# Splitting the values matmuls of an attention quad into two pieces, in a two-layer transformer kernel on one Trainium2 core

## The reference

```python
dots = jnp.einsum('bhid,bhjd->bhij', q, k) * scale
attn = jax.nn.softmax(jnp.where(mask, -jnp.inf, dots), axis=-1)
out = jnp.einsum('bhij,bhjd->bhid', attn, v)
x = _layernorm(x + out @ w_out + b_out)
x = _layernorm(x + ffn(x))
```

## Time and profile before

| what | us |
|---|---|
| runs of the kernel before | 1175.50, 1175.59, 1180.28 (median 1175.59) |
| the profiled execution | 1173.83 |
| its span, first to last instruction | 1172.1 |
| TensorE matmuls busy | 1027.9 |
| VectorE busy | 723.9 |
| ScalarE busy | 594.7 |
| GpSimd busy | 323.8 |

### The profile page before, as it was taken

One profiled execution on the slowest core, in us unless ns is written; L12 is line 12 of the kernel. 1 busy time (PEld: TensorE's weight loads), 2 busy tenths in 40 slices (PEclk: granted clock), 3 DMA queues, 4 the chain that ended last, 5 costly groups with the idle time before them and its releaser, 6 DMA issues. The chain is left out here.

```text
span 1172.1 us, 17910 instructions
## 1 busy us (share of the span) xinstructions
PE 1027.9 (88%) x6546; PEld 516.7 (44%) x6546; DVE 723.9 (62%) x1563; ACT 594.7 (51%) x1169; POOL 323.8 (28%) x391
## 2 busy tenths in 40 slices
PE   7947999999988899765779899999999988899996
PEld 4511233333324788742022333334333334488885
DVE  3767877777734655464878677777777724134322
ACT  3412667666665433234026576767777765523220
POOL 1041111111111343302135613315133150334331
PEclk9966999999999999878569999999999999999998
DMA  7585044444000000008922505235051000000001
GB/s 272 130 155 63 6 51 55 55 55 56 2 1 1 2 1 1 1 19 172 220 102 72 116 2 116 75 42 114 4 117 34 1 2 1 1 1 18 18 1 37
DMA packets 32980, 64.20 MB, mean 55 GB/s; under 512 B 6079, under 2 KB 22351, under 8 KB 30516
## 3 DMA queue, kind: packets, MB, share of 16 engines
q1 hardware_dynamic: 31004, 58.07, 24.9%
q0 software_dynamic: 1072, 3.80, 0.9%
q10 hardware_dynamic: 816, 1.18, 0.3%
HBM read 50.45 MB, written 12.32 MB: 54 GB/s over the span
## 5 line engine op out<-in xcount | busy, mean ns | idle before, releaser
L802 ACT ACTIVATE prob<-ps 128x512 f32<-128x512 f32 (+6 forms) x896 | 445.9, 535 | 306.1 <-PE ps L838 297.9
L838 PE MATMUL ps<-qop,kop 98*128 98x512 bf16 (+15 forms) x1376 | 311.8, 291 | 38.1 <-ACT prob L802 23.0
L824 PE MATMUL ps<-kop,qop 96*128 96x512 bf16 (+3 forms) x896 | 272.6, 380 | 53.1 <-DVE maxes L743 24.7
L838 PEld LDWEIGHTS ps<-qop,kop 107*128 107x128 bf16 (+2 forms) x1376 | 114.0, 98 | 311.7 <-ACT prob L802 236.7
L865 PE MATMUL ps<-prob,vst 128*32 128x512 f32 (+4 forms) x1792 | 212.1, 545 | 3.3 <-POOL prob L692 2.6
L743 DVE CUSTOM_DVE_ANT_0 attn<-ps,alibi_table 128x960 bf16<-128x960 f32 x128 | 148.0, 1156 | 86.6 <-PE ps L824 57.9
L692 POOL TENSOR_TENSOR prob<-prob,keep 128x384 int32<-128x384 int32 (+2 forms) x144 | 122.0, 849 | 276.1 <-ACT prob L802 273.5
L1207 PE MATMUL ps<-xs,ffn_parts 128*128 128x512 f32 x640 | 150.4, 392 | 4.5 <-DVE hf L1181 2.3
L743 DVE CUSTOM_DVE_ANT_0 tri<-ps,alibi_table 128x960 bf16<-128x960 f32 x128 | 147.6, 1153 | 3.0 <-PE ps L824 3.0
L824 PEld LDWEIGHTS ps<-kop,qop 96*128 96x128 bf16 x896 | 77.5, 100 | 143.4 <-DVE maxes L743 84.3
L1207 PEld LDWEIGHTS ps<-xs,ffn_parts 128*128 128x128 f32 x640 | 119.0, 188 | 29.7 <-DVE hf L1181 3.1
(11 more groups left out here) (97 smaller groups left out, 706.5 us busy)
## 6 DMA issues: line engine op xcount, KB each, us to landing
alibi_table<-in_table SPq DMA_DIRECT2D x32, 464.0 KB, 5.6
qop<-q_parts SPq DMA_DIRECT2D x96, 128.0 KB, 7.1
kop<-k_parts SPq DMA_DIRECT2D x48, 128.0 KB, 7.8
kop<-k_parts SPq DMA_DIRECT2D x48, 96.0 KB
q_parts<-qop SPq DMA_DIRECT2D x8, 384.0 KB, 3.0
q_parts<-kop SPq DMA_DIRECT2D x8, 384.0 KB, 6.5
x<-in_x SPq DMA_DIRECT2D x4, 512.0 KB, 7.2
out<-x SPq DMA_DIRECT2D x4, 512.0 KB, 2.9
```

The costliest lines, as they stand in the source:

```text
L802: nc.scalar.activation(prob[0:rows, q % 2, k % HG, lo % CH:lo % CH + hi - lo], ps[0:rows, T_BANK + k % 2, lo % CH:lo % CH + hi - lo], ACT. ...
L824: last = nc.tensor.matmul(ps[:, S_BANK + 2 * (k % S_SLOTS) + a // CH, a % CH:a % CH + b - a], qop[0:RD, par, h, i0:i0 + P], kop[0:RD, par, ...
L838: return nc.tensor.matmul(ps[0:rows, T_BANK + k % 2, a % CH:a % CH + b - a], lhs, rhs, start=start, stop=True, skip_group_check=True)
```

## The change

The values step of a quad is cut in two by query columns. `values0` does the first half of the columns, behind the third exponent step of the next quad and the score tiles due there, ahead of the fourth. It has the waits that the values step had: for the exponents, the masks and, where a sum is opened, the eviction. `values` does the second half where the values step stood, without a wait of its own, and raises `values_done`. The matmul that opens a sum, and the 64 small ones of the second layer, belong to the first piece. At the very end of a layer both pieces follow each other.

```diff
@@ -143,6 +143,10 @@
             upto = given_next + -(-(due_next - given_next) // (HG - h))
             steps += [("max", u, later) for u, later in stream_next[given_next:upto]]
             given_next = upto
+            if h == HG - 2 and n >= 1:
+                steps.append(("values0", n - 1, 0))
+            elif h == HG - 2 and late:
+                steps.append(("values0", nq - 1, -1))
         if n == 0 and late:
             steps += [(what, k, -1) for what, k in tail[:2]]
         if n == 1 and late:
@@ -161,7 +165,7 @@
         if n == rows_at and stream:
             steps.append(("rows", 0, 1))
     if last:
-        steps += [(what, k, 0) for what, k in tail]
+        steps += [("values0", nq - 1, 0)] + [(what, k, 0) for what, k in tail]
         steps = with_preparation(steps, nq)
     return steps
 
@@ -848,12 +852,14 @@
                         start = False
                 return last
 
-            def values(qd, par):
+            def values(qd, par, part):
 
                 half, kt = quads[qd]
                 lo, hi = columns_of(L, half, kt)
+                middle = (lo + hi) // 2
+                lo, hi = (lo, middle) if part == 0 else (middle, hi)
                 vt_ = kt if key_tile(L, kt)[1] == P else TB
-                opening = qd == 0 or quads[qd - 1][0] != half
+                opening = part == 0 and (qd == 0 or quads[qd - 1][0] != half)
                 uniform = opening and i == 1 and half == 0
                 if uniform:
 
@@ -901,6 +907,8 @@
                             pe.wait_ge(exp_done, n * NX + (k - 1))
                         shifted(k, b).then_inc(t_full, 1)
                     elif what == "values":
+                        values(k, b, 1).then_inc(values_done, 1)
+                    elif what == "values0":
                         half = quads[k][0]
                         if k > 0 and half != quads[k - 1][0]:
 
@@ -912,7 +920,7 @@
                         pe.wait_ge(exp_done, n * NX + HG * (k + 1))
                         if diagonal[k] is not None:
                             pe.wait_ge(masked, HG // MH * (n * upto[-1] + upto[k]))
-                        values(k, b).then_inc(values_done, 1)
+                        values(k, b, 0)
                     elif what == "norm":
                         pe.wait_ge(evicted, n * 2 + (k + 1))
```

## The result

The changed kernel took 1196.95, 1198.73 and 1210.12 us, against a median of 1175.76 us before: slower, ratio 1.0213 with a 95% interval of 1.0132 to 1.0295, which lies above 1 but does not settle whether it is 2% or more. A fourth run of 1263.25 us, at a mean granted clock of 0.813 where the others have 0.93 to 0.94, is left out of the ratio; with it the median of the runs is 1204.42 us. The profiled execution took 1196.95 us, 23.1 more than the 1173.83 of the one before, at the same granted clock (0.942 in both).

A forecast was written before the change was run, and what follows sets the result against it. TensorE was taken to bound both attention stages. Second layer +7.1 and first layer +14.3 made 21.4 us on the profiled 1173.83 us; with the runs' median 1.76 us higher, 1195.2 to 1197.0, stated as 1195, range 1181 to 1206.

The forecast's parts named there:

- The second edge: Extra entry to and exit from the values matmuls on TensorE: plus 0.10 and 0.14, about 0.24 us in every quad.
- What the piece fills: TensorE's wait for ScalarE between shifted 2 and shifted 3: minus 0.21 us, leaving +0.03 in an ordinary second-layer quad.
- The first layer, behind the third tile: Piece fills nothing behind the third score tile: nine quads (narrow last included) at 0.24, three at 0.03; 2.25 us a group.
- Group 6 of the first layer: First-layer group whose last four quads have no score tiles: allowed 6 x 0.24 and a little, 1.5 us.
- its last group: First layer's last group: about zero, with 0.5 us allowed for its 128-column quads.
- group 0 of the second layer: 32 score tiles over 13 quads, five quads with a values piece getting a third tile: plus 1.9 us.
- groups 1 to 6 of the second layer: Fourteen quads at 0.03 and two at 0.22 make 0.86 us a group: plus 5.2 us together.
- VectorE absorbs it: Rival, 0.13: VectorE limits first-layer quads with a third tile, so that layer costs 2 us, not 14.3; 1183 to 1185.
- The free edge: Rival, 0.08: the 0.14 and 0.10 us are not array time, only filling stays, about 31 us gained; 1143 us.
- The masks: Rival, 0.09: the piece waits for GpSimd in 136 masked quads, 0.1 us each, 14 us more; about 1208 us.

The follow-up runs named there:

- e1_adjacent: Changed kernel with both values pieces put together where the whole step stood, so cut but without a second entry and exit; 1177.03 us, ratio 1.001.
- e5_narrow_dummy: Kernel before the change plus one bf16 matmul per quad, 32 weight columns and 8 moving columns, ahead of shifted 1; 1198.32 us.
- e6_wide_dummy: Kernel before the change plus a tiny matmul per quad ahead of shifted 1, with the full key tile (128 columns, 64 in 64-row quads); 1187.62 us.
- e7_change_same_chip: Changed kernel unaltered, five rounds on the same chip as the version with uncut last groups; 1201.65 us, ratio 1.0216.
- e0_again: Changed kernel run again without an edit; median 1208.15 us in four runs, ratio 1.026.
- after: First profiled execution of the changed kernel itself, against the kernel before; 1196.95 us.

## Why the prediction was right, and where it was off

The prediction said slower, 1195 us in a range of 1181 to 1206, for a sum of 21.4 us on the profiled execution. The profiled execution of the changed kernel took 1196.95, 23.1 us more. In the comparison of five rounds the difference of the medians was 23.0 (1201.65 against 1178.69). The mechanism held; in two places errors of the parts cancelled, which was luck, and the clock was left out.

- **The second edge, 0.24 us.** In the 64-row quads of a second-layer group, which had almost no wait to fill, a quad became 0.26 and 0.24 us longer (0.22 in the sum), without a wait. The prediction took the price from how starts scale with width; that it is the change-over and not the cut is shown by `e1_adjacent` (no change in time) and `e5_narrow_dummy` against `e6_wide_dummy` (0.17 us a quad). The Trainium skill, page "TensorEngine Tiling (Array Packing)", section "Key Properties", says that a change of the tiling mode, not of the tile alone, drains TensorE. The two extra matmuls, alike but for their width, agree with it. Two pieces of values that follow each other pay no such time (`e1_adjacent`).
- **What the piece fills, 0.21 us.** Right in the second layer: the ordinary quads of a group became between 0.05 us longer and 0.03 shorter, 0.02 longer on average (0.03 predicted), a group gave +0.83 us (0.86), and the pieces of 256 columns were 0.57 us from start to next start.
- **The first layer, behind the third tile.** The nine quads of a group at 0.24 and three at 0.03 made 2.25 us, and 2.22 was measured. That the total fits so well is in part luck. In one group seven of the eight quads with a third tile became 0.25 us longer and the eighth 0.14; the narrow last quad, also counted at 0.24, gave 0.13; and of the three counted at 0.03 two gave 0.03 to 0.04 but the other narrow quad, at the end of the first half, 0.14. The prediction read TensorE's wait ahead of the third tile from one quad and took it for all eight; four have it. Its conclusion did not need it, since the piece stands behind the other waits too.
- **Terms that were mis-sized.** Group 6 of the first layer cost 1.94 us where 1.5 was allowed, its last group to the start of the second layer 1.64 where 0.5 was (0.92 of it in the group, the rest in the stretch behind it, for which the sum had nothing), and group 0 of the second layer 2.34 where 1.9 was. Together that is 2.0 us too little; groups 1 to 6 of the second layer, at 4.65 where 5.2 was allowed, take back 0.5. These are differences of the starts of the groups (shifted 0) in the two traces. Outside the sum lie 1.4 us less ahead of the first group and 1.9 us more from the start of the last group on. Each goes with a stretch of 3.4 us at 1.2 GHz that one of the two executions has and the other has not, so the profiled difference holds about 0.5 us of clock there.
- **VectorE absorbs it.** It fell as a whole: the wait of 0.46 us ahead of the third tile is still there and the groups are 2.2 us longer. VectorE was late because TensorE was, as its wait of 1.27 us for the first tile says. It holds in single quads: in the last quad of a first-layer group TensorE's wait for VectorE went from 0.38 to 0.13 us, and that quad paid only 0.13. Over the whole trace the matmuls of the score tiles wait 21.0 us for VectorE, where it was 24.7.
- **The free edge.** It fell: in the quads shown the tile after a 256-column piece comes 0.57 us behind its start, not 0.43. Pieces of one width that follow each other do not pay the time behind a piece (`e1_adjacent`: 1.00 us for two).
- **The masks.** They fell: 2.8 us of waits for GpSimd, where 2.6 was before.
- **What the prediction did not have.** Of the fourteen runs of the changed kernel in three comparisons seven lie in the stated range, 1196.95 to 1203.74 us, and seven above it. Two profiles differ by 8.5 us from the last group of the first layer on, with 20.5 us at half the clock in one; a third (`e7_change_same_chip`) has no such fall. The sum was made against one execution at a clock of 0.942, and said nothing of others. In `e0_again` the median of 1208.15 us lies beyond the range while the groups of its profile are those of the sum. Its other three runs have no profile; their mean clock, 0.930 and 0.931, makes the same cause likely. That the first comparison and the last came out inside the range is in that respect luck.

## What to carry to other kernels

Before a step is cut to fill a wait, price the change-over on both sides of the new piece against the wait: here the second piece's change-over cost 0.24 us and the wait that it filled was 0.21, and most of the first layer's pieces stood behind the waits instead of in one. A longest wait on an engine that is not the bound (ScalarE's 298 us) does not say where time is to be had; the bound engine's own waits, quad by quad, do, and steps moved whole or in part into them, with the score tiles shared out to suit, gave 2.6%.

## What the runs showed of the hardware that was not expected

- Cutting costs next to nothing: 1792 more matmuls (and as many weight loads), half the columns each, changed a group by 0.06 to 0.08 us (`e1_adjacent`), though each piece loads its weights anew.
- A bf16 matmul of 8 columns costs 0.17 us more when its weights are 32 columns wide than when they are 128, among 128-column matmuls. The switch has a price without float32 and without a long block of values, and in the kernel before already between tiles of 64 and 128 columns (0.11 and 0.09 us more from start to start).
- With the order of work unchanged, TensorE was granted 1.2 GHz for 20.5 us of the last first-layer group in one execution of the changed kernel and not at all in two others. Before it fell (354.6), TensorE went through shifted tiles and 64-column values pieces with waits for exponents between them, the last of 0.53 us; it did the same in `after`, the first of these. Where all runs of a kernel spread by half a per cent, the granted clock of each is the first number to compare.
